# Cross-attention and mixture of experts: tokens binned by pair of experts, rows scattered to the output, masks in 64x64 tiles

## What is computed

```python
# x, ctx: (128, 64, 128); mask: (128, 64), true for keys that don't count
q = (layernorm(x) + pe) @ Wq.T + bq
k = (ctx + pe) @ Wk.T + bk
v = ctx @ Wv.T + bv
scores = einsum('bhqd,bhkd->bhqk', qh, kh) * 8 ** -0.5
scores = scores - (mask[:, None, None, :] | causal) * 1e7
x = x + (softmax(scores) @ vh) @ Wo.T + bo

xt = layernorm(x).reshape(8192, 128)
probs = softmax(gelu(xt @ wg1 + bg1) @ wg2)           # 8 experts
top_vals, top_idx = top_k(probs, 2)                   # the two best, as gates
h = gelu(einsum('nd,edh->enh', xt, w_in))             # 128 -> 256
o = einsum('enh,ehd->end', h, w_out)                  # 256 -> 128
out = x + sum over the two experts of gate * o
```

## Time and profile before

| | us |
|---|---|
| median of 3 runs | 757.35 |
| lowest and highest of them | 752.66, 759.09 |
| the profiled execution, its own time | 764.19 |
| its span, first to last instruction | 762.3 |
| last residual of attention ends, in the span | 449.7 |
| last multiplication of a block ends | 721.4 |

### The profile page before, as it was taken

One profiled execution on the slowest core, in us unless ns is written; L12 is line 12 of the kernel. 1 busy time (PEld: TensorE's weight loads), 2 busy tenths in 40 slices (PEclk: granted clock), 3 DMA queues, 4 the chain that ended last, 5 costly groups with the idle time before them and its releaser, 6 DMA issues.

```text
span 762.3 us, 17286 instructions
## 1 busy us (share of the span) xinstructions
PE 567.0 (74%) x6054; PEld 386.6 (51%) x6054; DVE 463.8 (61%) x1511; ACT 352.8 (46%) x606; POOL 358.7 (47%) x438
## 2 busy tenths in 40 slices
PE   3588988988898898889888676362777868779800
PEld 1245654545554554555454365362666757668700
DVE  4478998887977887797868753252223223223374
ACT  2255876866666685666756343221222222224300
POOL 4122236474455546445633356565555565550075
PEclk9999999999999999999989769596898897889955
DMA  3363122122212212211110343242644443445498
GB/s 90 71 201 82 44 59 74 28 68 64 61 32 58 68 35 61 62 34 29 33 42 9 83 131 100 68 130 76 170 117 128 128 128 109 122 118 170 137 365 288
DMA packets 74470, 73.80 MB, mean 97 GB/s; under 512 B 22032, under 2 KB 61840, under 8 KB 74096
## 3 DMA queue, kind: packets, MB, share of 16 engines
q1 hardware_dynamic: 64160, 53.86, 26.5%
q0 software_dynamic: 8640, 18.37, 6.8%
q10 hardware_dynamic: 1584, 0.46, 0.2%
HBM read 44.99 MB, written 27.70 MB: 95 GB/s over the span
## 4 chain that ended last, share of the span: by engine, by line
PE 56%; issue 19%; DVE 11%; SPq 7%; POOL 4%; DMA 2%; ACT 1%; another core or an unknown queue 1%; ACTq 0%; POOLq 0%; DVEq 0%
PE probs_t L633 12%; PE bank L644 10%; PE probs_t L477 6%; PE scores L463 6%; SPq L281 4%; PE bank L495 4%; DVE smax L863 3%; PE bank L490 3%; POOL sm L1381 3%; PE scores L467 3%; DVE sm L867 3%; PE scores L624 3%; PE bank L504 2%; PE bank L443 2%; PE bank L534 2%
## 5 line engine op out<-in xcount | busy, mean ns | idle before, releaser
L1318 POOL DMA_INDIRECT routed_rows<-rows,pos x128 | 126.1, 985 | 136.6 <-DVE pos L963 94.1
L633 PE MATMUL probs_t<-xbT,wi 128*128 128x256 f32 x312 | 100.2, 450 | 76.1 <-issue 76.1
L1354 POOL DMA_INDIRECT expert_rows_by_token<-yb,token_row x118 | 113.0, 957 | 90.9 <-DVE token_row L1212 46.3
L1218 DVE TENSOR_TENSOR yb<-bank,gate 128x256 f32<-128x256 f32 x78 | 33.1, 425 | 182.2 <-PE bank L644 94.1
L810 ACT ACTIVATE hb<-probs_t 128x512 f32<-128x512 f32 x78 | 46.6, 597 | 163.5 <-PE probs_t L633 95.2
L633 PEld LDWEIGHTS probs_t<-xbT,wi 128*128 128x128 f32 x312 | 61.8, 220 | 89.2 <-issue 80.8
L863 DVE TENSOR_REDUCE smax<-scores 128x16 f32<-128x1024 f32 x64 | 78.0, 1219 | 40.7 <-PE scores L467 36.8
L771 ACT ACTIVATE pt<-probs_t 128x1024 f32<-128x1024 f32 x64 | 65.5, 1023 | 79.6 <-PE probs_t L477 76.4
L644 PE MATMUL bank<-wo,hb 128*128 x624 | 93.0, 298 | 0.0
L463 PE MATMUL scores<-kx,qT 64*64 64x512 f32 x512 | 73.9, 644 | 20.0 <-DMA kx<-kT 10.7
L644 PEld LDWEIGHTS bank<-wo,hb 128*128 128x128 f32 x624 | 86.7, 215 | 0.1
(11 more groups left out here) (131 smaller groups left out, 874.5 us busy)
## 6 DMA issues: line engine op xcount, KB each, us to landing
xb<-routed_rows SPq DMA_DIRECT2D x78, 138.0 KB
wi<-w_in SPq DMA_DIRECT2D x78, 128.0 KB
kx<-expert_rows_by_token SPq DMA_DIRECT2D x26, 256.0 KB
ctx_in<-ctx_t SPq DMA_DIRECT2D x16, 256.0 KB
x_all<-x SPq DMA_DIRECT2D x16, 256.0 KB
kx<-kT SPq DMA_DIRECT2D x256, 16.0 KB
out<-x_all SPq DMA_DIRECT2D x16, 256.0 KB
expert_rows<-yb SPq DMA_DIRECT2D x19, 128.0 KB, 2.0
```

The lines of the kernel that those rows point to most:

```text
L633: last = nc.tensor.matmul(UBK[b % 2][:, c * BLK:(c + 1) * BLK], wi[:, b % RX, c * P:(c + 1) * P], xbT[:, b % RH, :], start=True, stop=True)
L1318: nc.gpsimd.indirect_dma_start(out=rows_d, out_offset=bass.IndirectOffsetOnAxis(ap=pos[:, buf, k, u:u + 1], axis=0), in_=rows[:, buf, u, : ...
L1354: nc.gpsimd.indirect_dma_start(out=tok_d, out_offset=bass.IndirectOffsetOnAxis(ap=token_row[:, b % RY, u:u + 1], axis=0), in_=yb[:, b % RY ...
```

## The change

Tokens are sorted by the pair of experts that they go to. There are 28 pairs (`PAIRS`), each with a region; a token has one row, in one region. The row holds its normalised numbers, the attention result x, eight gates and the token's number: 265 words, 1060 bytes. A block is 128 tokens of one pair and computes both experts: four `up` products and both `down` sums. VectorE forms gate 0 times expert 0 plus x, then adds gate 1 times expert 1, and GpSimd scatters these final rows straight to the output; rows of padding carry numbers past the end and are dropped by a bounds check. So the final sum, its loads, gathers and stores are gone. There are no parts any more: all supertiles are routed first, then one table is made (`make_tables`: counts by rounding, a running sum in five shifted additions, three transposes on TensorE), 28 paddings go out from SyncE and ScalarE, and 91 blocks follow. The w_in of all experts is loaded once, and ScalarE copies the two that a block needs into place; the evacuation of the transposed rows moves from ScalarE to VectorE. The mask tile has a row for each of 64 queries in both halves, and four matmuls of 64x64 add it.

```diff
-PARTS = 2
-SPS = (13, 3)
-BT = 2
-BLK = BT * P
-NBS = tuple((KTOP * n + E * (BLK - 1)) // BLK for n in TPS)
-RW = D + E + 2
+PAIRS = [(a, b) for a in range(E) for b in range(a + 1, E)]
+NP = len(PAIRS)
+BLK = P
+NB = (N + NP * (BLK - 1)) // BLK
+RW = 2 * D + E + 1
+GB = 4
...
                 def load_mask(s):
-                    for b in range(2):
-                        src = mask[s * 2 * U:(s + 1) * 2 * U, :].rearrange("(u b) k -> b u k", b=2)[b]
-                        sp.dma_start(mask_in[b * L:(b + 1) * L, s % RING, :, :], src.partition_broadcast(L)
-                                     ).then_inc(s_m[s % RING], 16)
+                    sp.dma_start(mask_in[:, s % RING, :, :], mask[s * 2 * U:(s + 1) * 2 * U, :].partition_broadcast(P)
+                                 ).then_inc(s_m[s % RING], 16)
...
+        def pad_regions(engine, queue, bins):
+            for first in range(bins.start, bins.stop, NP // 4):
+                _, values = nc.values_load_multi_w_load_instructions(
+                    tails[0:1, first:first + NP // 4], engines=[engine], min_val=0, max_val=ROWS - BLK,
...
+                for k in range(NP // 4):
...
+                    queue.dma_start(rows_d[bass.ds(at, BLK), :], pad_c.ap()).then_inc(s_pad, 16)
...
                     for half in range(2):
-                        last = nc.tensor.matmul(S_bank[half][:, :].rearrange("p (h k) -> p h k", k=L), spread_s[:, :],
-                                         negmask[:, par, u, :].unsqueeze(1).broadcast_to([P, HH, L]),
-                                         start=False, stop=True)
+                        r = slice(half * 64, half * 64 + 64)
+                        for b in range(2):
+                            last = nc.tensor.matmul(S_bank[half][b * L:(b + 1) * L, :].rearrange("p (h k) -> p h k", k=L),
+                                                    spread_s[r, r], negmask[r, par, 2 * u + b, :].unsqueeze(1).broadcast_to([L, HH, L]),
+                                                    start=False, stop=True)
...
                 def up(b):
-                    for c in range(2):
-                        last = nc.tensor.matmul(UBK[b % 2][:, c * BLK:(c + 1) * BLK],
-                                                wi[:, b % RX, c * P:(c + 1) * P],
-                                                xbT[:, b % RH, :], start=True, stop=True)
+                    for j in range(2):
+                        for c in range(2):
+                            last = nc.tensor.matmul(UBK[b % 2][:, (2 * j + c) * BLK:(2 * j + c + 1) * BLK],
+                                                    wi[:, b % RH, j, c * P:(c + 1) * P], xbT[:, b % RH, :],
+                                                    start=True, stop=True)
...
+                def copy_w_in(b, experts):
+                    if b >= RH:
+                        act.wait_ge(s_up, b - RH + 1)
+                    for j in range(2):
+                        nc.scalar.copy(wi[:, b % RH, j, :],
+                                       wi_all[:, bass.ds(experts[j], 1), :].rearrange("p e h -> p (e h)")
+                                       ).then_inc(s_wi, 1)
+                for g, (first, n) in enumerate(GROUPS):
+                    experts = experts_of(g)
+                    for b in range(first, first + n):
+                        if b > 1:
+                            gelus(b - 2)
+                        copy_w_in(b, experts[2 * (b - first):2 * (b - first) + 2])
...
+                    nc.vector.tensor_tensor(coded[:, :, :], chosen[:, :, :], bits.unsqueeze(1).broadcast_to([P, U, E]),
+                                            ALU.mult).then_inc(s_coded, 1)
...
+                    nc.vector.reduce_sum(code[:, :], coded[:, :, :], AX).then_inc(s_code, 1)
+                    dve.wait_ge(s_code, r + 1)
+                    nc.vector.tensor_tensor(sel16[:, :, :], code[:, :].unsqueeze(2).broadcast_to([P, U, NP]),
+                                            codes.unsqueeze(1).broadcast_to([P, U, NP]), ALU.is_equal
...
                 def scatter_out(b):
                     pool.wait_ge(s_tok, b + 1)
                     pool.wait_ge(s_yb, b + 1)
+                    nc.gpsimd.indirect_dma_start(
+                        out=out, out_offset=bass.IndirectOffsetOnAxis(ap=token_row[:, b % RY:b % RY + 1], axis=0),
+                        in_=yb[:, b % RY, :], in_offset=None, bounds_check=N - 1, oob_is_err=False
+                        ).then_inc(s_ysc[b % RY], 16)
```

More of the change, by code:

```diff
@@ new lines, in build @@
+    fields = {
+        "region": np.arange(NP) * REG,
+        "experts": np.arange(E),
+        "bits": 2 ** np.arange(E),
+        "codes": 2 ** first_of + 2 ** second_of,
+        "to_next": np.concatenate([np.diff(first_of, append=0.0), np.diff(second_of, append=1.0)]),
+        "base": np.stack([BLK * np.arange(P), np.zeros(P), np.ones(P)], axis=1),
+        "row": row_no,
+        "token": tile_no * P + row_no,
+    }
+    fields = {k: np.broadcast_to(np.asarray(v, np.float32), (P, np.shape(v)[-1])) for k, v in fields.items()}
@@ new lines, in build @@
+    ends = np.cumsum([v.shape[1] for v in fields.values()])
+    place = {k: slice(int(e) - v.shape[1], int(e)) for (k, v), e in zip(fields.items(), ends)}
+    NR = int(ends[-1])
+    routing_c = nc.inline_tensor(np.ascontiguousarray(np.concatenate(list(fields.values()), axis=1)), name="routing")
+    region_c = nc.inline_tensor(np.ascontiguousarray(fields["region"]), name="region_starts")
+    next_c = nc.inline_tensor(np.ascontiguousarray(fields["to_next"]), name="expert_steps")
+    padding = np.zeros((BLK, RW), np.float32)
@@ L321, in _ @@
                              w_out.rearrange("e (c p) d -> p (e c) d", p=P)).then_inc(s_wo, 16)
[L322 to L334 removed]
+                sp.dma_start(wi_all[:, :, :], w_in.rearrange("e d h -> d e h")).then_inc(s_wo, 16)
                 def body(s, i, par):
@@ L365, in load_group @@
                     for k in range(n):
                         b = first + k
-                        r = b % RX
-                        at = values[2 * k]
-                        expert = nc.s_assert_within(
-                            values[2 * k + 1], 0, E - 1,
-                            skip_runtime_bounds_check_because="made on the chip, zero for blocks that hold no rows")
                         if b >= RX:
                             sp.wait_ge(s_bt, b - RX + 1)
-                            sp.wait_ge(s_gm, b - RX + 1)
-                            sp.wait_ge(s_tok, min(b - RX + 1, NBS[0]))
@@ L414, in _ @@
[L414 to L424 removed]
+                            sp.wait_ge(s_yb, b - RX + 1)
@@ L428, in _ @@
+                        sp.dma_start(xb[:, b % RX, :], rows_d[bass.ds(values[k], BLK), :]).then_inc(s_xb[b % RX], 16)
+                sp.wait_ge(s_tails, 1)
+                pad_regions(mybir.EngineType.SP, sp, PAD_SP)
+                sp.wait_ge(s_tabd, 1)
+                for g in range(len(GROUPS)):
+                    load_group(g)
+                for i in range(RY):
+                    sp.wait_ge(s_ysc[i], 16 * len(range(i, NB, RY)))
             @block.tensor
@@ L680, in _ @@
                             transposes(b + 2)
-                        down(b, experts[b - first])
-                        last_gates(b)
+                        down(b, experts[2 * (b - first):2 * (b - first) + 2])
             @block.scalar
@@ L824, in _, with experts_of @@
-                xbT_evac(0)
-                gelus(0)
-                xbT_evac(1)
-                for b in range(NB):
-                    if b + 1 < NB:
-                        gelus(b + 1)
-                    if b + 2 < NB:
-                        xbT_evac(b + 2)
-                    last_gates(b)
+                def experts_of(g):
+                    first, n = GROUPS[g]
+                    _, values = nc.values_load_multi_w_load_instructions(
+                        expert_table[0:1, first:first + n, :].rearrange("p b c -> p (b c)"),
+                        engines=[mybir.EngineType.Activation], min_val=0, max_val=E - 1,
+                        skip_runtime_bounds_check_because="made on the chip, zero and one for blocks that hold no rows")
+                    return values
```

711 lines of the change are left out of this document (248 added, 463 removed).

## The result

The changed kernel took 625.76 us (median of 4 executions, 623.75 to 626.70), the kernel before 757.99 beside it (median of 4): a ratio of 0.826, 95% interval 0.822 to 0.831. 645 had been predicted. That is one chip. On two later chips the kernel before itself takes 620.5 to 622 us, and on the one of them where the changed kernel ran too, the ratio is 1.000; on two others the kernel before takes 764. Single executions far from the rest of their kernel (680.8 and 1242.6 us of the kernel before on chip B) are left out of the ratios.

A forecast was written before the change was run, and what follows sets the result against it. Trains of GpSimd scatters were taken to stall attention and blocks. Last residual at 390, plus 38 for the hole, 216 for blocks, 5 for the end: span 649, time 651, lowered by 6.8 to 645; range 615 to 705.

The forecast's parts named there:

- a train of GpSimd scatters: Attention and expert blocks: scatters issued in a row cost some 4 us in each supertile, over 1 us in each block.
- Two commands in a row cost nothing: Attention: the stall shows only in trains; two scatter commands in a row have no cost that the profile shows.
- Rival (a): Attention and blocks: the stall follows each scatter, not trains; half is kept, time 720; chance 0.22.
- (b): Expert blocks: ScalarE's weight copies, GELU and register work become the bound at 2.4 us; +15 to 30, 668; chance 0.10.
- (c): Attention and blocks: the stall goes with bytes and DMA queues; supertiles keep 26.26 us, blocks 3.49, time 805; chance 0.05.
- (d): Attention: the four mask matmuls run one after another, +0.42 us for 64 tiles without the gain, 679; chance 0.05.
- The supertile: Attention, twelve supertiles: 26.26 us falls to 22.3, from 21.0 + 1.2 + 0.5 less 0.4; 47.5 us in all.
- VectorE's +0.95 against half of TensorE's -0.85: Each supertile: VectorE's added mask and selection work counted in full, TensorE's mask saving by half, net 0.5 us.
- The hole: Between attention and experts: 38 us without an expert matmul for routing, padding and first load; bounds 28 and 50.
- The blocks: Expert stage: 91 blocks at 2.03 us, 185, plus register loads 20, half clock 5, rest of the stall 6: 216 us.
- The register loads: Every fourth block, ScalarE and TensorE read eight register values: 0.9 us for 23 groups, 20 us (nothing to 45).
- The end: After the last block: one VectorE multiply, one scatter and its landing, 5 us, replacing the final sum from 722 to 763.

The follow-up runs named there:

- before_in_pairs: The kernel before with its eight scatter commands a supertile issued in pairs, one pair a tile, instead of four, two and two; 718.95 us against 764.17.
- old_mask: The changed kernel with the mask as before: two 128x128 matmuls a tile, negmask at half size, two mask loads a supertile; 620.32 us, kernel before 620.97.
- one_train: The changed kernel with a supertile's four scatter commands issued one behind the other at its first tile; 620.70 us, kernel before 620.97.

## Why the prediction was right in its number and where it was not

**The result** lies in the range (615 to 705) and on the side that had 0.95, and it is 19 us below the 645. That it came out faster is in part luck of the chip: on chip B the same two programs differ by nothing, and 620 us is there the time of both. The forecast never asked whether the stall belongs to the program. The cause it gave holds for stalling chips, as far as C and D speak for the first one; as a statement about the program it does not.

**"I read a train of GpSimd scatters as the cause."** Shown for stalling chips, with a condition that the profile of one execution could not show. The cleanest run is before_in_pairs: same commands and bytes, beside the kernel before on one chip, 6% less. The kernel with the trains put back takes 100 us more on D than on A (780 against 680), but most of that is in the blocks, where commands were added too. On calm chips the same trains in attention cost nothing. "Two commands in a row cost nothing" was too much: on chip C some 0.9 us a supertile was left with pairs alone, 23.18 against the 22.26 of the kernel before on chip B. And a train of four costs 1.6 us a supertile in the changed kernel on D, where some 4 us for the train and pairs of the kernel before had been read; what makes up the rest is open.

**Rival (a), each scatter,** falls: with single commands the changed kernel took 23.02 us a supertile on the first, stalling chip, 22.99 (97.82 to 373.73) on the calm chip B, and without any 22.95 on chip A. **(b), ScalarE,** did not bound the changed kernel: 1.2 us of TensorE's idle time for weight copies. **(c), bytes,** falls with before_in_pairs, same bytes and 45 us less, and with blocks of 1.90 us. **(d)** falls with the trace of the changed kernel, where the four mask matmuls together take 0.40 us and the two took 0.60:

```profile
379.64 0.40 PE L383 MATMUL scores<-negmask,spread_s 64*64 64x512 f16 x4
```

**The supertile: 22.3 predicted, 23.02 measured,** 8.6 us over twelve. The base was right: 21.0 + 1.2 = 22.2, and the kernel before takes 22.26 where nothing stalls. The step that failed is the trade of VectorE's +0.95 against half of TensorE's -0.85, and the 0.4 for fewer descriptors. In the changed kernel VectorE is the bound: it is busy for 96% of a supertile, and old_mask, which takes 0.26 us from it and gives TensorE about 0.8 us more, is 0.26 us a supertile faster. So TensorE's gain counts for nothing there. That it was so in the kernel before as well (97% busy on chip B) is read from the share and not shown by a run. VectorE's own time grew by 0.65 us (0.966 x 22.26 to 0.962 x 23.02), and the supertile by 0.76. The first three supertiles gained 5.5 us (supertile 3 begins at 96.12 instead of 101.65) where 3 was counted, and the last residual came at 396.7 instead of 390.

**The hole: 38 predicted, 35.7 measured.** The terms as given, 17 + 16 + 3.5, add up to 36.5 and not to 38. Padding was issued for 13.2 us where 11.6 was counted; the steps ahead of it took 16 us (396.74 to 412.81) for 17.

**The blocks: 216 predicted, 178 measured** (432.46 to the end of the last down matmuls, 610.3). This is the largest miss, in four terms. The register loads, 20 us, cost nothing: blocks follow each other at 1.90 us whether or not they load registers, and in 166 us TensorE is busy for 164.8. The block of 2.03 was 1.90, since eight passes need 0.89 us and not 0.96: 12 us. The half clock cost 2 us where 5 stood, in the first two blocks (the up groups behind them start 2.73 and 2.70 us later instead of 1.90). The rest of a stall, 6 us, was none. That is 41 us less; 3 us came on top that had no term: the wait between first transpose and first up matmul, the one block of 3.3 us, and the last block's way through ScalarE.

**The end: 5 predicted, 11.7 measured** (610.3 to 622.0). The work itself is done in time: two scatters queue behind the last down matmuls and the last packet lands at 614.0 us, 3.7 us behind them. The other 8 us is a term that the sum lacked: the records of the trace have a DRAIN of GpSimd at the close of the program from 611.8 to 621.7 us, and the span ends with it. In the kernel before, such a DRAIN lay beside the gathers of the final sum (740.8 to 761.5, last packet at 761.5) and showed nowhere.

Together +6.7 - 2.3 - 38 + 6.7 = -27 on the span; the 6.8 us by which the profiled execution of before lay above the median had no counterpart after (623.75 against a median of 625.76), and so 645 became 626. The number is closer than its largest terms, since the misses have both signs.

**What did not move.** The scatter took 982 ns in the dense blocks, 1004 in attention [0.985 and 0.957 in rows 6]. By the rule on shared SBUF interfaces (the Trainium skill, GPSIMD Engine Reference, Key points) VectorE instructions with two SBUF inputs would contend with it. The four means lie within 0.05 us of each other, so in these rows the effect is small if there is one. The stall of the stalling chips works the other way round, TensorE stopping beside GpSimd's trains, and that rule does not explain it here, since the same instructions on a calm chip don't stall.

**What stays open:** which property makes a chip stall, and by which path a train reaches TensorE's issue. Instruction loading does not look like the path: the kernel before loads 50 pieces of 16 KB with a median of 1.15 us on the first chip and 1.08 on B. Chip A was calm twice, 47 minutes apart, and C stalled in between; but each stalling chip was used on one occasion only, so that it is the chip and not the occasion is likely and not shown. And what the changed kernel itself is worth on a stalling chip other than the first.

## What to carry to other kernels

A gap that the profile ascribes to nobody ("issue") may belong to the chip and not to the program: before building a rewrite on it, run the unchanged kernel on a second chip. Spacing GpSimd's indirect commands, one per piece of other work, is a cheap insurance: on a calm chip it made no difference in the changed kernel (one_train), and pairs instead of a train of four took 6% off the kernel before on a stalling one. And find which engine is nearly full with the stalls gone: a saving on the other one (here the mask on TensorE) gave nothing in the changed kernel on a calm chip and 2% in the kernel before on a stalling one. Kernel and chip differ between these two, so whether the stalls alone make that difference was not tested.

## What was not expected of the hardware

One program, 757 to 764 us on three chips and 620 to 622 on two, with nearly the same durations of single instructions (GELU 597 ns, scatter 985 and 987, mask matmul 395 and 388; the up matmul, at a lower granted clock, 450 and 412). The added time lies beside trains of GpSimd's indirect commands, in gaps and in matmuls that follow each other more slowly. SyncE's register moves, which the timeline leaves out, show it in the records of the trace too: 26 of its 450 register and semaphore operations last 0.5 to 0.9 us, most around 0.7, in the kernel before on the first chip, none on chip B.

A direct DMA of GpSimd's queue landed 8.2 us behind its issue (median of seven), so a third queue that looked free brought nothing.
